# Two-layer graph attention: the next batch's mask made in the fourth slot, its diagonal at the batch's turn, x loaded ahead

## What is computed

```python
mask = (adj > 0) | eye(N)                       # layers 1 and 2
def gat_layer(x, mask, W, a_src, a_dst, bias):
    xl = x @ W                                  # per head
    e = leaky_relu(xl @ a_src [source] + xl @ a_dst [target], 0.2)
    attn = softmax(where(mask, e, -1e9), axis=sources)
    return attn.T @ xl + bias
h = gat_layer(elu(gat_layer(x, mask, W1, ...)), mask, W2, ...)
x = layernorm(x + h)
Wh = x @ W;  e = leaky(Wh @ a1 [i] + Wh @ a2 [j])
attention = softmax(where(adj > 0, e, -9e15), axis=i)      # layer 3: no diagonal
out = layernorm(x + leaky(attention @ Wh))
```

## Time and profile before

| | |
|---|---|
| median of three runs | 949.05 us |
| profiled execution, its span | 949.35 us, 947.1 us |
| TensorE busy | 876.1 us (92% of the span) |
| VectorE busy | 753.7 us (80%) |
| ScalarE busy | 686.9 us (73%) |
| GpSimd busy | 257.2 us (27%) |
| chain that ended last, by engine | PE 35%, DVE 31%, ACT 24%, issue 8% |
| `make_mask` L944 | 16 times, 1202 ns mean |
| `set_diag` L420 | 16 times, 1185 ns mean |
| `x_lo` L949 | 16 times, 1218 ns mean |

### The profile page before, as it was taken

One profiled execution on the slowest core, in us unless ns is written; L12 is line 12 of the kernel. 1 busy time (PEld: TensorE's weight loads), 2 busy tenths in 40 slices (PEclk: granted clock), 3 DMA queues, 4 the chain that ended last, 5 costly groups with the idle time before them and its releaser, 6 DMA issues.

```text
span 947.1 us, 17311 instructions
## 1 busy us (share of the span) xinstructions
PE 876.1 (92%) x6220; PEld 815.5 (86%) x6220; DVE 753.7 (80%) x1908; ACT 686.9 (73%) x1274; POOL 257.2 (27%) x244
## 2 busy tenths in 40 slices
PE   5777889999999999999999999999999999999887
PEld 3676879998998989899898989989898998989775
DVE  6757687878888887888888788888878888887666
ACT  2566858778686887868688786868878686887653
POOL 1001001124231342423133242313324231331512
PEclk9897989999999999999999999999999999999999
DMA  7403030301203040120303013030301201000001
GB/s 200 128 1 90 1 89 1 87 4 34 79 19 94 1 108 5 34 79 21 93 1 109 4 35 78 22 91 1 112 2 35 77 24 23 1 24 1 23 1 67
DMA packets 62747, 45.03 MB, mean 48 GB/s; under 512 B 35780, under 2 KB 54340, under 8 KB 62664
## 3 DMA queue, kind: packets, MB, share of 16 engines
q1 hardware_dynamic: 62664, 43.93, 16.5%
HBM read 27.14 MB, written 8.39 MB: 38 GB/s over the span
## 4 chain that ended last, share of the span: by engine, by line
PE 35%; DVE 31%; ACT 24%; issue 8%; POOL 0%; DMA 0%; DVEq 0%; SPq 0%; POOLq 0%; ACTq 0%
DVE junk L888 10%; PE bU L530 7%; PE bU L509 6%; PE bG L602 6%; PE bG L616 6%; ACT att L720 6%; ACT att L705 6%; ACT x L732 5%; DVE y_lo L925 3%; DVE att L939 3%; PE bB L469 3%; DVE low L901 3%; DVE y L913 3%; ACT att L724 2%; DVE stats L978 2%
## 5 line engine op out<-in xcount | busy, mean ns | idle before, releaser
L509 PE MATMUL bU<-val,att 128*128 128x129 f32 x2048 | 249.5, 275 | 3.6 <-DVE att L939 3.6
L888 DVE CUSTOM_DVE_ANT_0 junk<-mask_t,bA,val 128x512 bf16<-128x512 bf16 x320 | 219.8, 743 | 35.5 <-PE bA L469 33.0
L509 PEld LDWEIGHTS bU<-val,att 128*128 128x128 f32 x2048 | 241.4, 192 | 6.0 <-issue 3.6
L939 DVE SCALAR_TENSOR_TENSOR att<-mask_n,att 128x2048 f32<-128x2048 bf16 x78 | 178.8, 2293 | 81.4 <-ACT att L720 81.0
L705 ACT ACTIVATE att<-bB,val 128x512 f32<-128x512 f32 x320 | 203.0, 708 | 3.1 <-PE bB L469 3.1
L720 ACT ACTIVATE att<-att 128x2048 f32<-128x2048 f32 x78 | 151.5, 1942 | 0.6
L772 ACT COPY val<-bG 128x524 f32<-128x524 f32 x64 | 38.7, 605 | 104.3 <-PE bG L616 104.3
L520 PE MATMUL bU<-val,att 128*128 128x257 f32 x480 | 109.8, 381 | 1.9 <-DVE att L935 1.2
L530 PE MATMUL bU<-val3s,att 128*128 128x256 f32 x480 | 109.2, 381 | 1.7 <-DVE res L969 0.2
L732 ACT ACTIVATE x<-bU,zinv 128x128 f32<-128x128 f32 x256 | 73.4, 375 | 47.6 <-DVE zinv L919 47.6
L380 POOL TENSOR_SCALAR var_eps<-moments 128x4 f32<-128x4 f32 x29 | 5.7, 195 | 368.0 <-DVE moments L981 368.0
(11 more groups left out here) (116 smaller groups left out, 1628.7 us busy)
## 6 DMA issues: line engine op xcount, KB each, us to landing
adj_in<-in_adj_dram SPq DMA_DIRECT2D x16, 1024.0 KB, 5.7
x_in<-in_x_dram SPq DMA_DIRECT2D x16, 512.0 KB, 6.7
out_dram<-act SPq DMA_DIRECT2D x14, 512.0 KB, 2.9
mask_t<-mask_n SPq DMA_TRANSPOSE x64, 2.5
att<-in_L_gnn_W_dram SPq DMA_DIRECT2D x4, 128.0 KB, 3.2
att<-in_L_gnn_W_dram SPq DMA_DIRECT2D x1, 512.0 KB, 7.6
out_dram<-x_in SPq DMA_DIRECT2D x1, 512.0 KB, 3.0
w<-in_L_gnn_W_dram SPq DMA_DIRECT2D x1, 256.0 KB, 7.2
```

Of the source, the lines that this page charges most:

```text
L509: ins = nc.tensor.matmul(to[:, (d % 2) * FX:(d % 2 + 1) * FX], p[:, s, d * P:(d + 1) * P], val1[u.batch % 2][:, s, u.index // 2, values], ...
L888: nc.vector.tensor_tensor_reduce(junk[:, b] if u.row else att[u.slot % 3][:, b], mask_t[u.batch % 4][:, b], bA[:], 1.0, a_col(u, b) if u.r ...
L939: nc.vector.scalar_tensor_tensor(flat(p), mask_n[u.batch % 3][:, 0:NB * N], BIG, flat(p), ALU.add, ALU.min)\
```

## The change

`make_mask(n + 1)` moves from VectorE's slot 0, where it stood ahead of `x_low`, to the end of slot 3 of the same batch, behind `elu`. `set_diag` moves from GpSimd's slot 2, where batch n set the diagonal of batch n+1 between the last residual and the bias, to slot 0 of batch n itself, behind `scale_3`. On SyncE the load of x stands ahead of the transposes of the mask and no longer behind the load of adj. The first mask (batch 0) is made as before. TensorE's and ScalarE's instructions and their order stay.

```diff
@@ SyncE
             for n in range(-1, B):
+                if 2 <= n + 2 < B:
+                    load_x(n + 2)
                 if n + 1 < B:
                     turn_mask(n + 1)
                 if 1 <= n + 2 < B:
                     load_adj(n + 2)
-                if 2 <= n + 2 < B:
-                    load_x(n + 2)
                 if n >= 3:
                     store(n - 3, range(NB))
@@ GpSimd
                 if pos == 0 and 0 <= n - 3:
                     scale_3(n - 3)
+                if pos == 0 and 0 <= n < B:
+                    set_diag(n)
                 if pos == 2 and 0 <= n - 2 < B:
                     norm_scale(n - 2, 0, moments1, var1, rstd1)
                 if pos == 2 and 0 <= n - 2 < B:
                     pool.wait_ge(x1n_done, (n - 1) * NB)
                 if pos == 2 and 0 <= n - 3 < B:
                     residual_2(n - 3)
-                if pos == 2 and 0 <= n + 1 < B:
-                    set_diag(n + 1)
                 if pos == 3 and 0 <= n - 1 < B:
                     add_bias_2(n - 1)
@@ VectorE
                 elif pos == 0 and n + 1 < B:
-                    make_mask(n + 1)
                     x_low(n + 1)
...
                 if older:
                     elu(older)
+                if pos == 3 and 1 <= n + 1 < B:
+                    make_mask(n + 1)
```

## The result

The changed kernel takes 961.77 us, the median of 4 runs (960.24 to 963.36), and the kernel before, run beside it, 950.02 us (948.87 to 952.58). The ratio is 1.0116, with a 95% interval of 1.0098 to 1.0135. It is slower, by 1.2%. The forecast was 958.3 us within 951 to 961.5. The median lies 0.3 us above that range, but the kernel before also ran 0.97 us longer beside it than the 949.05 us on which the forecast stands; 1.0116 x 949.05 = 960.1 us lies within it. The profiled execution took 960.76 us, 11.41 more than the profiled one before, and its span is 958.5 us against 947.1.

A forecast was written before the change was run, and what follows sets the result against it. TensorE was nearly full (53.45 of 55.2 us a batch), so edits count only through waits on the chain. 12 x 0.47, 12 x 0.26 and 0.5 made 9.2 us slower: 958.3 us forecast, range 951 to 961.5.

The forecast's parts named there:

- A: VectorE's slot 3: bias starts earlier without the diagonal ahead, `low` is held less; gain 0.53 us a batch.
- B: End of VectorE's slot 3: the mask comes in between `y` and `zinv`, delaying ScalarE's L732; cost 1.00 us a batch.
- C: VectorE's slot 0: the mask goes out ahead of `x_lo`, which then waits for `x_hi`; gain 0.24 us a batch.
- D: Slot 0: the diagonal on GpSimd (L420) holds VectorE's `y` (L913); cost 0.50 us a batch.
- the bound of 0.64: Slot 3: most that an earlier `low` can return through TensorE's `bB`, from its 0.43 us wait and cold 0.65 against 0.44.
- The expected successor: Slot 0: with the mask gone, `x_lo` waits next for ScalarE's `x_hi`, so only 0.24 us come back.
- The prediction's case against the rule: A `y` started at 502.22 inside GpSimd's L389 (499.71 to 502.79) took its plain 0.68 us, so not every row holds.
- first batches 2.8 - 2.3 = 0.5: Batches 0 to 2: the mask costs 2.8 us in slot 3 (0.6 for batch 2), 2.3 return in slot 0.
- Rival 1: Slot 0: GpSimd's L420 does not hold `y`; 3.3 us slower, 952.3 us; chance 0.15.
- rival 2: ScalarE between L732 and slot 4's exp: the mask is hidden in slot 3; not slower, 946.3 us; chance 0.09.
- rival 3: Slot 3: earlier bias brings nothing because TensorE or L939 decides; 6.4 us missing, 964.7 us; chance 0.08.
- Rival 4: Slot 0: the mask's transposes land late and VectorE waits; 970 us and more; chance 0.02.

The follow-up runs named there:

- fourth: The kernel before with only GpSimd's diagonal moved from slot 2 to slot 4: 943.52 us, ratio 0.9929.
- fifth: The changed kernel with a filler of the diagonal's form added on GpSimd in slot 2, ahead of the bias: 966.58 us, ratio 1.0167.
- second: The changed kernel with the mask moved from the end of VectorE's slot 3 to slot 4, ahead of L939: 942.61 us, ratio 0.9914.
- third: The changed kernel with both the mask and the diagonal moved to slot 4: 937.15 us, ratio 0.9865.
- first: The changed kernel with the diagonal moved from GpSimd's slot 0 to slot 4, one batch ahead: 955.28 us, ratio 1.0054.
- sixth experiment: The changed kernel with a second mask, written to a spare buffer, in VectorE's slot 0 ahead of `x_lo`: 973.49 us, ratio 1.0240.
- repeat: The changed kernel itself measured once more, nothing edited: 961.26 us, ratio 1.0111.
- x behind: The changed kernel with the load of x back behind the transposes and the load of adj: 961.79 us, ratio 1.0113.

## Why the prediction was right, and where its sizes were off

The direction, the four places and the period were right: 55.9 us was forecast and 55.90 measured. Each term, with the experiment that isolates it:

| place | predicted, us a batch | measured | from |
|---|---|---|---|
| A, `low` held for less time | -0.53 | -0.64 alone, about -0.54 with the mask in slot 3 | fourth, fifth |
| B, mask ahead of `zinv` | +1.00 | +1.10 (with A's 0.64) | second |
| C, mask out of slot 0 | -0.24 | -0.23 | fourth less third: 54.56 - 54.33 |
| D, diagonal holds `y` | +0.50 | +0.49 | first |
| sum | +0.73 | +0.72; +0.70 between the kernels | |

**A and B.** The 0.53 and the 1.00 go together, and so do 0.64 and 1.10. In the kernel before, L939 was a floor under `y` that left 0.53. Where no mask stands behind `y`, the path that counts is ScalarE's `e` and L732, and it keeps the whole 0.64. The net of A and B, 0.47, was measured as 0.46: each alone was 0.1 too small, for one reason, and in the net this cancels. One reading under the bound of 0.64 was mixed: the 0.65 us of `bB` is a row of the timeline, the 0.44 a stretch of the chain, and in the timeline the set at 488.40 us, without a stall, takes 0.60. What comes back is the wait of 0.43, 0.17 by which `bB` then overlaps the matmuls ahead of it, and 0.05 of its own length.

**C.** The expected successor was there: `x_hi`, with 0.79 us of idle time in front of `x_lo`. The mask had been nearly free in slot 0. That a mask can stand for nothing in slot 4, behind `zinv` and ahead of an exp, was not asked of the prediction; the second experiment shows it.

**D.** `y` ended 0.55 us behind L420, 0.13 less than its own length; by the same reckoning as at A the hold ends about that much before the holder's row does. The Trainium skill, SBUF — State Buffer, section "Who interferes with whom", has the first to issue hold the port for its whole duration. The sixth experiment agrees that the wait can be nearly the whole length of the holder, 1.05 us of 1.15. It also shows that the start of a row does not tell who is first.

The prediction's case against the rule, L389 at 499.71 us, was read too simply: that row is 3.08 us long where the median of this form is 1.22 us. VectorE's L939, with two inputs in SBUF, had started ahead of it:

```profile
499.41 2.29 DVE L939 SCALAR_TENSOR_TENSOR att<-mask_n,att 128x2048 f32<-128x2048 bf16 x1 [1.91 <-ACT att L720]
```

So 1.86 us of the row are L389's own wait, and it worked from about 501.57 to 502.79. The `y` at 502.22 still lies in that part and was not held, so the doubt that the prediction drew from it stands. Clearer is a `low` inside an L389 of plain length (496.05 to 497.27); it took its plain 0.17 us:

```profile
497.12 0.17 DVE L901 SCALAR_TENSOR_TENSOR low<-top,val 128x4 f32<-128x4 f32 x1
```

**Where the numbers fell short.** 9.2 us were forecast between the profiled executions and 11.4 measured. By the offset between the two profiles at matching instructions the 11.4 are 1.7 ahead of any moved instruction, 1.1 from there to the first `x_lo` of the steady part, 7.6 over eleven periods and 1.0 behind the last one. The last two are 8.6 where twelve times 0.73 are 8.8. The other two:

The 1.7 us have nothing to do with the change. VectorE's first maxima start at 29.71 us here, and at 28.00 in the kernel before:

```profile
29.71 0.75 DVE L888 CUSTOM_DVE_ANT_0 junk<-mask_t,bA,val 128x512 bf16<-128x512 bf16 x1 [2.24 <-issue]
```

```profile
28.00 0.75 DVE L888 CUSTOM_DVE_ANT_0 junk<-mask_t,bA,val 128x512 bf16<-128x512 bf16 x1 [1.32 <-issue]
```

By then nothing that was moved has run, but blocks of TensorE's L616 in the start-up ran at 0.42 us a matmul in place of 0.28. From this point to the end of the span the changed kernel takes 928.8 us in this profile, 928.7 with the x load moved and 927.9 in the repeat, against 919.1 before: 8.7 to 9.7 us more, around the forecast 9.2.

The 1.1 us, for which the forecast has 0.5, are the step that failed: "first batches 2.8 - 2.3 = 0.5". It left two things out or too small. First, place D works in batches 0 and 1 too, as GpSimd is free early there and the diagonal waits for the transposed read to be over. GpSimd, then VectorE:

```profile
65.23 1.16 POOL L420 TENSOR_TENSOR mask_n<-mask_n,ident_big 128x512 bf16<-128x512 bf16 x1 [41.31 <-DMA mask_t<-mask_n]
```

```profile
65.68 1.26 DVE L913 SCALAR_TENSOR_TENSOR y<-e,x 128x512 f32<-128x512 f32 x1
```

The `y` was held for 0.58 us, and in batch 1 for 0.37 (a row of 1.05 us, beside an L420 that starts at 112.55); twelve holds were counted and fourteen came. Second, the mask of batch 2 cost more than the 0.6 taken between 0 and 1.1: the instruction of TensorE's path ahead of it (`y_hi`) stood 1.98 us later than in the kernel before, and L732 behind it 3.10 us later, so it cost 1.12 us, the upper end. L732 behind the masks of batches 0 and 2:

```profile
58.52 1.14 ACT L732 ACTIVATE x<-bU,zinv 128x128 f32<-128x128 f32 x4 [2.55 <-DVE zinv L919]
...
158.07 1.14 ACT L732 ACTIVATE x<-bU,zinv 128x128 f32<-128x128 f32 x4 [0.99 <-DVE zinv L919]
```

Against these 1.5 us stand about 0.9 given back between 127 and 138 us. The stretches there, of the kernel before and then of the changed one (the last three numbers are the granted clock, the DMA share and GB/s):

```profile
128.00:136.00 8.00, 4.67 (x24) 4.43 (x23) 7.44 (x21) 1.18 (x2) 0.32 (x2) 0.67 0.74 201
```

```profile
130.00:138.00 8.00, 4.77 (x31) 4.43 (x30) 7.42 (x19) 2.08 (x3) 0.00 (x0) 0.85 0.24 66
```

The granted clock was 0.67 before and 0.85 after, so TensorE spent less of this stretch at 1.2 GHz, the lower of its two levels. Most of the 0.9 can be read from the lengths of the matmuls. In the chain the four `bB` there are, before and after:

```profile
131.75 1.12 PE bB L469 x4
```

```profile
134.57 0.65 PE bB L469 x4
```

They start 2.82 us apart. Over them and the first matmuls behind them, which also ran shorter (the first L616 0.28 us in place of 0.42), the distance falls to 1.98 us without any wait. So 0.84 us came back because the same matmuls ran shorter. What set the clock there was not tested.

Two smaller shifts cancel: 0.26 us more near 44 us, where two L616 took 0.42 and 0.37 us in place of 0.28, and 0.25 less at the `x_lo` of 180.68 us, which is a C of the steady part.

**What stays open.** The runs' medians lie 11.7, 12.3 and 11.8 us above those of the kernel before (changed kernel, x behind, repeat); the profiles without the start-up give 8.7 to 9.7. The last two intervals begin at 1.0088 and 1.0085, 8.4 and 8.1 us, and so hold 9.2; that of the first begins at 1.0098, 9.3 us. Whether the changed kernel draws slow start-up blocks more often than the kernel before, or by chance, one profile of each run can't tell. The pair that is most alike, one slow block each, is the kernel before and the one with x behind: 959.15 - 949.35 = 9.8 us between the profiled executions.

Rival 1 fell by the first experiment (0.49 a batch came back when the diagonal left), rival 2 by the second and by the 0.99 us in front of L732, rival 3 by the fourth and fifth. Rival 4 showed no wait in any profile.

## What to carry to other kernels

Ask of each slot what ends last there before an instruction is moved: the same mask of 1.2 us cost 1.10 us a batch between `y` and the reciprocals that ScalarE waits for, 0.23 where it filled most of a wait, and nothing half a slot later. Look for instructions of one engine that are longer than their kind's median: the idle columns don't show a held port, and here both the gain and a third of the loss were in such rows. Count the start of the program and its end with the same care as the steady part, since there a moved instruction can meet neighbours that it never meets later.

## What the runs showed of the hardware

A wait for the port stands inside the row of the instruction that waits, as time busy and not as idle time: `y` took 1.16 and 1.73 us, and `low` 0.93, 1.91 and 2.02.

The hold did not go to the one whose row began first. With `y` at 525.05 us and the diagonal at 525.08, `y` waited 1.05 us; this was so, within 0.01 us, in all twelve batches of the steady part of the sixth experiment. The row of `y_lo` ahead of it lasts to 525.13, so `y` may have started work only behind the diagonal's 525.08, and been second after all; no run separates the two. How far ahead `y` would have to be is not shown.

Not every GpSimd instruction of this kind holds VectorE. The forms with two tensor inputs did (L406 of 2.36 us, L420 of 1.16). L389, with one tensor input and two columns as scalars, did not: a `low` inside it took 0.17 us, and an L939 that started 0.9 us behind another (499.41 against 498.51), with 0.3 us of it left, took its plain 2.29 us.

In the other direction VectorE did hold these forms of GpSimd. L939 stretched one L389 of each last norm from 1.22 to 3.1 us. A mask on VectorE stretched four L414 from 1.85 to 2.66 us in the kernel before and in the sixth experiment, with one tensor input on either side.

The start-up is not the same from run to run. Matmuls of one form (L616) came in blocks at 0.28 to 0.29 us or at 0.42, in code that no edit touched. The changed kernel, early and a little later:

```profile
19.76 0.42 PE L616 MATMUL bG<-w_hi,x_hi 128*128 128x262 f32 x1
...
23.78 0.28 PE L616 MATMUL bG<-w_hi,x_hi 128*128 128x262 f32 x1
```

The kernel with x behind, early:

```profile
19.56 0.28 PE L616 MATMUL bG<-w_hi,x_hi 128*128 128x262 f32 x1
```

One slow block puts VectorE's first maxima at 28.0 to 28.2 us, two at 29.7, three at 31.1 and four at 32.5 to 32.6, about 1.45 us for each. The kernel before had one, the changed kernel two and its repeat four, which is 2.9 us between two executions of one program. Rows of 0.42 us are the length that L616 also had at 133 us in the kernel before, at a granted clock of 0.50; here the trace has 1.00 (15.00 to 18.40 and 19.40 to 22.40 us of the changed kernel), so the granted clock of the trace does not show the slow blocks.
